# Three moves in a transformer-layer kernel on Trainium2: operand loads paced by chunk, attention transposes placed before the down projection, projection statistics one batch further ahead

## The reference

```python
x = x + attention(layernorm(x))       # 16 heads of 8 channels, relative positions clipped to +-20
#   scores = (q.k + q.rel_k[clip(pos_k - pos_q)]) / sqrt(8); softmax over keys
#   out    = (attn.v + attn.rel_v[clip(...)]) @ Wo.T + bo
x = x + ffn(layernorm(x))             # ffn: (silu(x Wg.T) * (x Wu.T)) @ Wd.T, hidden 384, int weights / 127
```

## Time and profile before

| | us |
|---|---|
| median of 3 runs | 1425.4 (1424.68 to 1428.78) |
| the profiled execution, its own time | 1427.91 |
| its span, first to last instruction | 1426.0 |
| busy PE / PEld / DVE / ACT / POOL | 1281.4 / 941.6 / 948.1 / 758.8 / 550.8 |
| mean granted TensorE clock | 0.96 |
| share of 16 DMA engines, SP's queue | 19.1% |

### The profile page before, as it was taken

The page is one execution under the profiler, slowest core; times in us unless marked ns, Lnnn a source line. Parts: engine busy times, 40 slices in busy tenths (PEclk is TensorE's granted clock), DMA queues, the critical chain, the costliest instruction groups (busy, mean ns, idle before and its releaser), DMA issues. The chain is left out here.

```text
span 1426.0 us, 67609 instructions
## 1 busy us (share of the span) xinstructions
PE 1281.4 (90%) x30680; PEld 941.6 (66%) x30688; DVE 948.1 (66%) x1844; ACT 758.8 (53%) x1413; POOL 550.8 (39%) x983
## 2 busy tenths in 40 slices
PE   4377669999999999999999999999999999889998
PEld 2244337777777777777777776777777777656665
DVE  6499777776766766766767667667767676055554
ACT  4276526565655655655656556556556566422222
POOL 4376533543435343435334353434344343022221
PEclk9689859999999999999999999999999999989999
DMA  4445420202020202112020202021120200122321
GB/s 138 114 168 183 155 57 8 53 23 63 9 64 20 53 20 55 25 48 53 20 63 13 64 20 53 21 54 30 43 55 21 64 9 9 41 60 67 89 67 45
DMA packets 101541, 79.08 MB, mean 55 GB/s; under 512 B 13256, under 2 KB 97032, under 8 KB 101256
## 3 DMA queue, kind: packets, MB, share of 16 engines
q1 hardware_dynamic: 101256, 74.77, 19.1%
HBM read 45.90 MB, written 27.26 MB: 51 GB/s over the span
## 5 line engine op out<-in xcount | busy, mean ns | idle before, releaser
L1039 DVE TENSOR_REDUCE b_mx<-b_a 128x1 f32<-128x512 f32 x1024 | 658.7, 685 | 239.2 <-PE b_a L806 233.8
L1000 ACT ACTIVATE b_p<-b_s 128x512 f32<-128x512 f32 x1024 | 569.8, 595 | 417.5 <-PE b_s L847 332.8
L897 PE MATMUL b_pv<-b_p,vg 128*16 128x128 f32 x8192 | 286.8, 275 | 0.0
L770 POOL TENSOR_TENSOR qd<-q,one 48x512 bf16<-48x512 bf16 x256 | 266.1, 1040 | 30.1 <-POOLq L286 5.3
L747 POOL TENSOR_TENSOR b_np<-vg,one 128x16 bf16<-128x16 f32 x192 | 39.1, 264 | 581.1 <-DVE b_mx L1039 570.3
L847 PE MATMUL b_s<-qd,z 112*128 112x32 bf16 (+1 forms) x6016 | 248.9, 189 | 2.8 <-issue 2.8
L806 PE MATMUL b_a<-k,q 48*128 48x512 bf16 x1024 | 203.6, 394 | 28.2 <-DVE b_mx L1039 12.6
L847 PEld LDWEIGHTS b_s<-qd,z 112*128 112x128 bf16 x6016 | 206.0, 99 | 15.2 <-issue 5.3
L897 PEld LDWEIGHTS b_pv<-b_p,vg 128*16 128x16 f32 x8192 | 196.3, 96 | 21.1 <-issue 0.2
L832 PE MATMUL b_s<-q,k 54*128 54x64 bf16 (+3 forms) x4608 | 187.8, 201 | 6.8 <-issue 3.3
L832 PEld LDWEIGHTS b_s<-q,k 54*128 54x128 bf16 (+1 forms) x4608 | 126.2, 95 | 92.2 <-PE b_s L832 29.2
(11 more groups left out here) (125 smaller groups left out, 1312.7 us busy)
## 6 DMA issues: line engine op xcount, KB each, us to landing
x<-in_x SPq DMA_DIRECT2D x32, 256.0 KB, 3.1
scratch_qop<-a_parts SPq DMA_DIRECT2D x16, 384.0 KB, 2.5
scratch_kop<-a_parts SPq DMA_DIRECT2D x16, 384.0 KB, 3.1
k<-scratch_kop SPq DMA_DIRECT2D x32, 192.0 KB
q<-scratch_qop SPq DMA_DIRECT2D x32, 192.0 KB
scratch_v<-a_vr SPq DMA_DIRECT2D x16, 256.0 KB, 3.2
k<-scratch_kop SPq DMA_DIRECT2D x32, 128.0 KB
q<-scratch_qop SPq DMA_DIRECT2D x32, 128.0 KB
```

What stands on the lines that cost most here:

```text
L770: nc.gpsimd.tensor_tensor(dst, src, one, ALU.mult).then_inc(s["qd_ready"], 1)
L897: nc.tensor.matmul(PV[32 * a:32 * a + V16, g * P:(g + 1) * P], v[:, 0 if t <= i else 1, t, h, :], PR[at.c % 2][:, t, h, :], start=(t == 0 ...
L1000: nc.scalar.activation(out, src, ACT.Exp, scale=SCALE).then_inc(s["p_ready"], 1)
L1039: nc.vector.tensor_reduce(MX[v.c % 2][:, h:h + 1], PA[(n + hp) % NBANK][:, :], AX_X, ALU.max, negate=True).then_inc(s["a_used"], 1)
```

## The change

Three parts. (1) In stage 1 x is loaded, and its statistics and deviations taken, three batches ahead and not two (x of batch 2 is loaded among the constants); ACT normalises batch at+2 ahead of evacuating the projections of at+1. (2) In stage 2 each of the 12 operand loads waits for a chunk of its own: six in unit i = 0 (first half of the heads), then v and guards at chunk 6, six in unit i = 1. (3) In stage 3 the attention transposes of at+2 and their copy come before the down projection and the copy of the rows.

```diff
@@ stage_project, sync
-            for dst, src in late:
+            for n, (dst, src) in enumerate(late):
                 sp.dma_start(dst, src).then_inc(s["late"], 16)
+                if n == 9:
+                    sp.wait_ge(s["xn"], 1)
+                    load_x(at0(2))
...
-                if at.plus(2).exists():
-                    sp.wait_ge(s["xn"], at.count(1, 1))
-                    load_x(at.plus(2))
+                if at.plus(3).exists():
+                    sp.wait_ge(s["xn"], at.count(1, 2))
+                    load_x(at.plus(3))
@@ stage_project, scalar
                 part(at, 1, 2, pk).then_inc(s["ksplit"], 1)
+                if at.plus(2).exists():
+                    normalised(at.plus(2))
                 if at.plus(1).exists():
                     projected(at.plus(1))
-                if at.plus(2).exists():
-                    normalised(at.plus(2))
@@ stage_project, gpsimd and vector
-            deviation(at0(0))
-            deviation(at0(1))
+            for b in range(3):
+                deviation(at0(b))
...
-                if at.plus(2).exists():
-                    deviation(at.plus(2))
+                if at.plus(3).exists():
+                    deviation(at.plus(3))
...
-            for b in range(2):
+            for b in range(3):
                 statistics(at0(b))
...
-                if at.plus(2).exists():
-                    statistics(at.plus(2))
+                if at.plus(3).exists():
+                    statistics(at.plus(3))
@@ stage_attend, sync
+                def chunk(c):
+                    sp.wait_ge(s["s_ready"], at.count(NSR, 2 * c + 1))
+
                 if ahead and i == 0:
-                    sp.wait_ge(s["s_ready"], at.count(NSR))
-                    operands(first, range(0, 3))
+                    for c in range(3):
+                        chunk(c)
+                        operands(first, range(c, c + 1))
                 if ahead and i == 1:
-                    operands(first, range(9, 12))
+                    for c in range(3):
+                        chunk(c)
+                        operands(first, range(c + 6, c + 7))
                 if at.plus(1).exists():
                     guard_rows(at.plus(1))
                 if ahead and i == 0:
-                    operands(first, range(3, 6))
+                    for c in range(3, 6):
+                        chunk(c)
+                        operands(first, range(c, c + 1))
+                    chunk(6)
                     sp.wait_ge(s["w_ready"], at.count(1))
                     load_values(sp, k, d, at.it * 2 + at.c // T + 1, (at.c // T + 1) % 2)
-                    operands(first, range(6, 9))
+                if ahead and i == 1:
+                    for c in range(3, 6):
+                        chunk(c)
+                        operands(first, range(c + 6, c + 7))
@@ stage_output, tensor (scalar likewise: transposed_attention ahead of transposed_rows)
+                if at.plus(2).exists():
+                    attention_transposes(at.plus(2))
                 for c in range(FC):
                     down(at, c)
                 if after.exists():
                     row_transposes(after)
-                if at.plus(2).exists():
-                    attention_transposes(at.plus(2))
```

More of the change, by code:

```diff
@@ L1228, in step @@
                     nc.scalar.activation(sg[:, c, :], PG[(at.c * FC + c) % 2][:, :], ACT.Silu).then_inc(s["silu"], 1)
+                if at.plus(2).exists():
+                    transposed_attention(at.plus(2))
                 if at.plus(1).exists():
                     transposed_rows(at.plus(1))
-                if at.plus(2).exists():
-                    transposed_attention(at.plus(2))
             run_all(step, 2, B)
```

## The result

| | before | after |
|---|---|---|
| median of 4 runs, us | 1426.12 (1424.68 to 1428.78) | 1446.53 (1440.65 to 1448.83) |
| span of the profiled execution, us | 1426.0 | 1444.1 |
| mean granted TensorE clock | 0.960 | 0.958 |

The ratio is 1.0135, with a 95% interval of 1.01 to 1.0169.

A forecast was written before the change was run, and what follows sets the result against it. The prediction took PE to bound stage 2 (busy 1010.8 of 1071.5 us) and DVE to become stage 1's bound. Its terms, -6 - 27 + 21 - 10 = -22 us, gave 1403 us from 1425.4, range 1382 to 1420.

The forecast's parts named there:

- Part 1, stage 1: Stage 1: statistics a batch ahead let DVE win 60% of its 10 us idle time, a gain of 6 us.
- The 2.4 us line: Stage 1: ACT's normalising, PE's transposes and the copy stood in one line of 2.4 us, forecast to leave the path.
- The stall for x: Stage 1: DVE's 18.9 us wait for x behind batch 0's 14 loads was forecast to stay, with no gain.
- Part 3, stage 3: Stage 3: earlier transposes remove PE's wait for `c_aT`, 14 steps x 0.73 = 10 us gain; bounds 5 and 11.
- Part 2a, the bursts gone: Stage 2: spreading the operand loads ends delayed instruction fetches, a gain of 27 us; bounds 15 and 30.
- the ruler: Stage 2: guard-row issues, once a unit, used to time batches: 65.18 us each before, 63.0 + 1.5 forecast.
- no backlog in front of PE's instructions: Stage 2: a 192 KB load needs 0.9 us of a 2 us chunk at 225 GB/s, so fetches are not delayed.
- rival C: Stage 2: the pauses stay, or every load costs its share wherever it stands; 1417 to 1430 us, chance 0.10.
- Part 2b, the loads come later: Stage 2: q loads behind the guard rows make PE wait 1.5 us a batch, 14 times, 21 us lost.
- B: Stage 2: q loads run at 48 GB/s or below, PE waits 3.6 us 14 times, 50 us; 1432 us, chance 0.07.
- A: Stage 2: the q loads land in time; -43 us, or 1383 us, chance 0.20.
- D: Stages 1 and 3: the change doesn't do what it says there; -9 us, or 1416 us, chance 0.11.

The follow-up runs named there:

- e6_qearlier: The change with the last k load of unit 1 moved behind the three q loads, so these go one chunk earlier; 1402.41 us, ratio 0.9833.
- e5_qsplit: The change with the 192 and 128 KB q loads issued as 3 and 2 loads of 64 KB at the same chunks; 1403.75 us, ratio 0.9844.
- e10_qlater: The change with the three q loads of unit 1 waiting one chunk longer, at chunks 4, 5 and 6; 1467.72 us, ratio 1.0287.
- e2_part2: The kernel before with only the paced operand loads of stage 2, one to a chunk; 1471.04 us, ratio 1.0306.

## Why the prediction was wrong, step by step

**Part 1, stage 1 (6 us; measured 8.3 by the medians, 8.5 in the profile).** Right. The 2.4 us line is gone: PE's wait for `a_xn` is one of 15.5 us at the start where it was 15 with 39.1. In its place PE now waits for DVE's `a_gr` in every step (36.5 us, 15 times, in the list above). DVE is the bound, at 96% in the steady part, as the windows show beside the earlier trace rows:

```profile
68.00:153.00 85.00, 63.35 (x355) 41.87 (x354) 81.93 (x209) 59.70 (x117) 61.34 (x79) 0.96 0.50 172
```

60% of DVE's idle time was too cautious. The stall for x stays, 17.2 us of DVE behind the same 14 loads, as said.

**Part 3, stage 3 (10 us, measured 12.4, above the upper bound of 11).** Right in kind; the term was read from the wrong column. PE's timeline at a border of steps answers to the earlier trace rows:

```profile
1306.40 0.60 PE L1180 MATMUL c_pt<-ident,c_xn 128*128 128x128 f32 x4
1306.83 1.06 PE L1172 MATMUL c_py<-wo,c_aT 128*128 128x128 f32 x8
1307.73 1.07 PE L1189 MATMUL c_pg<-c_xnT,wg 128*128 128x512 f32 x2
```

Matmuls start before the one ahead ends: `c_py` now follows `c_pt` by 0.43 us though that is 0.60 long. The gap before was therefore not the 0.73 us of idle time but 1309.18 - 1307.86 (start of `c_pa`) less 0.44, so 0.88. The full steps show it: their period fell from 10.59 to 9.65 us, by 0.94, of which 0.88 is this gap. Over the stage, 13 such steps give 12.2, the last but one 1.4, and the first step, which is 1.3 us longer, takes that back.

**Part 2a, the bursts gone (27 us).** The direction was right, the size was not: 14 us in the change itself (12 in unit 1, 2 in unit 0, with the spread of the ruler some 5 either way) and, by the medians, 8 to 10 with q first. The step that failed is "no backlog in front of PE's instructions". That a load of 192 KB to a chunk would not delay a fetch was argued from the rate of k loads. In the runs each group of transfers near unit 1 has a price, the value loads too. They stayed where they were, and in unit 0 the pacing did not hold either: in batch 3 q, values and guard were issued from 402.12 to 405.9 us, right behind the guard rows, and a pause followed:

```profile
402.12 2.60 SPq L230 DMA_DIRECT2D q<-scratch_qop  x3
404.98 0.47 SPq L235 DMA_DIRECT2D vr<-scratch_v  x1
405.50 0.43 SPq L236 DMA_DIRECT2D vg<-scratch_guard  x1
```

```profile
410.98 0.26 PE L847 MATMUL b_s<-q,k 51*128 51x64 bf16 x5 [1.65 <-issue]
```

That was rival C, and half of it came true. The total at stake, 30 us by the ruler, was about right: 26 by the medians.

**Part 2b, the loads come later (21 us).** This is the step that decided. The place, the number and the releaser were as foretold: 14 waits at the first row pair of each third unit. The term was mis-sized twice. First the lateness: taken 1.5 us, measured 2.64, 37 us in all. To be 1.5 us late the forecast needed 8.0 us from the guard rows to usable q, 1.9 of fixed time and 6.1 of moving. The packets of the 14 batches give 9.1 from the first issue: 1.6 to the first packet, 6.9 for all 384 KB (57 GB/s; the window with 82 above counts the writes of finished rows and an instruction packet too), 0.7 from the last packet to PE. So the fixed time was short by 0.4 us and the moving time by 0.8. The row of 68 GB/s shows the pace of the 192 KB load, with a share of 3.2 engines, and the 128 KB load moves at 47 to 48, with a share of 2.2; choosing the time "near the end of the row that was read in mid-series" took too little of the second. The fastest batch, the third, took 5.9 us for all three loads, near the forecast's lower end of 5.8; the slowest took 7.8. Second, and not in the sum at all: behind eight of the 14 stalls PE worked at the lower clock, so that unit 2 grew by 3.8 us on average for 2.6 us of waiting, 16 us in all. Bound and rivals priced a stall at its own length.

**The rivals.** B, the slower one, is what happened, though not by its mechanism (48 GB/s throughout): its price of 50 us was met by 37 + 16 = 53, which is a coincidence. Its threshold of 3.1 us of lateness was too high, since a stall of 2.6 us already cost 3.8. A and D fell: q did not land in time, and stages 1 and 3 gained more than forecast. Two slips of arithmetic change nothing: half of C's chance is 0.05, so that "faster" comes to 0.88, and A's sum gives 1382.

The sum: -8.5 in stage 1, +39.0 in stage 2 (-14 + 53), -12.4 in stage 3, so +18.1, the difference of the two spans. Against the forecast of -22 that is 40 us off: 13 from 2a, 16 from the lateness, 16 from the clock, less 5 from the other stages.

## What to carry to other kernels

A load that is spread out for the sake of others is also issued later: write down for the last of them when it is issued (behind everything ahead of it in its queue), how many engines carry it, and when it is read, and put the narrow, slow loads first. Price a stall of TensorE at more than its length, as it can cost the clock too; here stalls of 2.6 us cost 3.8 on average. And count every transfer that stands near an engine with dense code, not only the bursts, for its instructions come by the same DMA engines.

## What was unexpected of the hardware

**Whether a stall costs the clock does not follow from its length alone.** Unit 2's extra time over 14.38 us beside the idle time in it, as means: 0.6 for 0.5 (`e6_qearlier`), 1.3 for 1.1 (`e5_qsplit`), 3.9 for 2.6 (the change), 5.2 for 3.3 (`e10_qlater`). On average longer stalls cost more than their length, but in the change, `e2_part2` and `e10_qlater` each stall either keeps the clock and costs about its length (0.1 to 0.4 us more), or loses it and costs 1.5 to 3.0 us more, and no length separates the two. Within the change, the batch in which PE stalled for 1.86 us kept the clock:

```profile
428.00:432.00 4.00, 4.00 (x156) 3.06 (x155) 3.06 (x5) 2.17 (x4) 3.62 (x5) 1.00 0.01 4
```

In `e2_part2` a stall of 1.76 us lost it:

```profile
708.52 0.39 PE L818 MATMUL b_a<-k,q 48*128 48x512 bf16 x2 [1.76 <-DMA q<-scratch_qop]
```

```profile
708.50:712.50 4.00, 3.98 (x80) 2.56 (x84) 2.13 (x4) 1.49 (x3) 3.54 (x6) 0.57 0.02 4
```

and in `e10_qlater` one of 2.80 us, the only one of its 14, kept it:

```profile
983.90 0.39 PE L821 MATMUL b_a<-k,q 48*128 48x512 bf16 x2 [2.80 <-DMA q<-scratch_qop]
```

```profile
983.90:987.90 4.00, 4.00 (x154) 3.10 (x154) 2.98 (x5) 2.17 (x4) 3.69 (x4) 1.00 0.01 4
```

**A pause has a length of its own behind the fetch.** From the landing of the instruction packet to PE's next matmul lie 1.3 to 2.0 us in all 69 cases; none is shorter.

What stays open: why the packets of the same three q loads take 5.9 us in one batch of the change and 7.8 in another (instruction packets and the writes of finished rows fall into that time, and no run took them away), what decides whether a stall costs the clock, and which transfer it is that delays a fetch; the runs show only that less of them near unit 1 means less of it.
